# The low halves of the expert rows of three batches: from a GpSimd subtraction to a TensorE difference that ScalarE copies out

## The reference, cut to what matters

```python
h = h + attention(layernorm(h))                     # 4 x 384 x 192
x2 = layernorm(h)                                   # the expert rows
logits = x2.reshape(1536, 192) @ router_w.T         # 8 experts
probs = softmax(logits); topk_probs, topk_idx = top_k(probs, 2)
u = silu(einsum('th,eih->tei', x2, w1)); outs = einsum('tei,ehi->teh', u, w2)
h = h + sum over the two chosen experts of outs * balanced weight
```

## Time and profile before

| what | value |
|---|---|
| time, median of 3 runs | 314.09 us (311.51 to 314.11) |
| the profiled execution | 313.65 us |
| its span, first to last instruction | 311.9 us |
| what lies around the span | 1.75 us |
| mean granted TensorE clock | 0.911 |
| TensorE busy | 241.0 us (77%) |
| VectorE busy | 213.9 us (69%) |
| ScalarE busy | 178.5 us (57%) |
| GpSimd busy | 114.9 us (37%) |

### The profile page before, as it was taken

One profiled execution on the slowest core, in us unless ns is written; L12 is line 12 of the kernel. 1 busy time (PEld: TensorE's weight loads), 2 busy tenths in 40 slices (PEclk: granted clock), 3 DMA queues, 4 the chain that ended last, 5 costly groups with the idle time before them and its releaser, 6 DMA issues.

```text
span 311.9 us, 7415 instructions
## 1 busy us (share of the span) xinstructions
PE 241.0 (77%) x2435; PEld 173.0 (55%) x2436; DVE 213.9 (69%) x650; ACT 178.5 (57%) x418; POOL 114.9 (37%) x150
## 2 busy tenths in 40 slices
PE   2896977486675878898979987399999999999400
PEld 1365357243444556675667776147777677777300
DVE  2076777789998756867969999556566566566546
ACT  1167035167878989897897265045565456555222
POOL 5000005134453033030403031556768677773400
PEclk9999997569999799899899999569999999999955
DMA  6992001400000000303000021112122111110076
GB/s 173 301 246 55 2 1 30 172 1 1 3 0 3 0 2 2 104 2 103 3 2 30 14 64 49 35 48 61 61 62 72 47 62 54 42 38 32 5 243 211
DMA packets 13390, 19.01 MB, mean 61 GB/s; under 512 B 3451, under 2 KB 11138, under 8 KB 12850
## 3 DMA queue, kind: packets, MB, share of 16 engines
q1 hardware_dynamic: 10018, 13.90, 14.8%
q0 software_dynamic: 3024, 4.73, 5.1%
q10 hardware_dynamic: 320, 0.01, 0.1%
HBM read 14.69 MB, written 5.41 MB: 64 GB/s over the span
## 4 chain that ended last, share of the span: by engine, by line
PE 42%; DVE 25%; ACT 14%; DMA 6%; issue 6%; SPq 4%; POOL 1%; DVEq 0%; POOLq 0%; ACTq 0%
PE bank L989 4%; PE bank L1002 3%; PE bank L1004 3%; PE bank L1003 3%; DMA qk<-in_w1b 3%; PE bank L974 3%; DVE third_place L1426 3%; PE bank L978 2%; PE bank L976 2%; PE bank L977 2%; PE bank L975 2%; PE bank L960 2%; ACT at_half L1156 2%; DMA v<-y_rows 2%; PE bank L651 2%
## 5 line engine op out<-in xcount | busy, mean ns | idle before, releaser
L1239 ACT ACTIVATE qk<-bank 128x512 f32<-128x512 f32 x31 | 18.5, 597 | 49.6 <-PE bank L978 49.6
L564 POOL DMA_INDIRECT qk<-x_rows,tok_row x32 | 34.5, 1078 | 19.4 <-issue 8.8
L571 POOL DMA_INDIRECT y_rows<-qk,dst_row x31 | 31.4, 1011 | 20.2 <-DVE qk L1792 13.4
L1002 PE MATMUL bank<-wx,qk 128*128 x124 | 30.5, 246 | 0.6 <-DVE qk L1786 0.5
L1004 PE MATMUL bank<-wx,qk 128*128 x124 | 30.5, 246 | 0.0
L1003 PE MATMUL bank<-wx,qk 128*128 x124 | 30.5, 246 | 0.0
L1786 DVE COPY qk<-bank 128x512 f16<-128x512 f16 x31 | 13.2, 425 | 24.8 <-PE bank L989 24.8
L1476 DVE SCALAR_TENSOR_TENSOR at_half<-bank,at_half 128x384 f16<-128x384 f32 x48 | 25.1, 548 | 4.4 <-ACT at_half L1156 4.2
L1780 DVE TENSOR_TENSOR qk<-qk 128x512 f16<-128x512 f32 x31 | 21.4, 692 | 7.9 <-ACT qk L1240 7.9
L1156 ACT ACTIVATE at_half<-bank 128x384 f16<-128x384 f32 x48 | 21.3, 511 | 2.8 <-PE bank L802 2.8
L989 PEld LDWEIGHTS bank<-ident,qk 128*128 128x128 f16 x248 | 16.6, 99 | 7.7 <-DVE qk L1780 1.1
(11 more groups left out here) (317 smaller groups left out, 706.2 us busy)
## 6 DMA issues: line engine op xcount, KB each, us to landing
early<-in_w SPq DMA_DIRECT2D x4, 768.0 KB, 4.6
qk<-in_w1a SPq DMA_DIRECT2D x2, 1024.0 KB, 6.2
qk<-in_w1b SPq DMA_DIRECT2D x4, 512.0 KB, 10.2
x_rows<-xr SPq DMA_DIRECT2D x4, 288.0 KB, 2.3
v<-y_rows SPq DMA_DIRECT2D x4, 288.0 KB, 4.9
qk<-y_rows SPq DMA_DIRECT2D x4, 288.0 KB, 5.3
out<-hr SPq DMA_DIRECT2D x4, 288.0 KB, 2.7
at_half<-in_wq SPq DMA_DIRECT2D x1, 704.0 KB
```

The lines of the kernel that those rows point to most:

```text
L564: pool.indirect_dma_start(xg[:, i % 4, :], None, x2_dram, bass.IndirectOffsetOnAxis(ap=tok_row[:, i:i + 1], axis=0), bounds_check=NTOK - 1 ...
L571: pool.indirect_dma_start(y_dram, bass.IndirectOffsetOnAxis(ap=dst_row[:, i:i + 1], axis=0), ye[:, i % 4, :], None, bounds_check=2 * NTOK ...
L1002: pe.matmul(o_, actT[:, k, 0, c], w[:, W2H + d:W2H + d + D], start=(m == 0), stop=False)
```

## The change

Only the low halves of batches 1 to 3 are formed in another way. Batch 0 stays on GpSimd.

- VectorE writes a negative identity `minus16` once, at `t == 1` of the attention loop.
- TensorE has `rows_low(b)`: into banks 6 and 7 of PSUM it multiplies the float32 rows by the float32 identity, and adds the high half times the negative identity. It waits for ScalarE's high halves, and from batch 2 on for ScalarE's copy of the batch ahead.
- ScalarE has `rows_low(b)`: it copies both banks as float16 into the low columns of `xr`. Its order becomes: high 1, high 2, low 1, low 2, high 3, the exponential, low 3, clear `xg`.
- The two runs of 50 matmuls of `keep_busy` become 24 + 14 and 20 + 18, around the new ones, and write to bank 2 instead of bank 7.
- SyncE waits for ScalarE's copies for batches 1 to 3.

```diff
@@ SyncE
-                sp.wait_ge(s_xlo_ready, 2 * (b + 1))
+                if b == 0:
+                    sp.wait_ge(s_xlo_ready, 2)
+                else:
+                    sp.wait_ge(s_xdiff_ready, 2 * b)
@@ GpSimd
-            for b in range(1, B):
-                rows_low(b)
@@ TensorE
-            keep_busy(50)
+            def rows_low(b):
+                pe.wait_ge(s_xhi_ready, 2 * (b + 1))
+                if b >= 2:
+                    pe.wait_ge(s_xdiff_ready, 2 * (b - 1))
+                xrow, xf = xr[:, b % 2 * CT:(b % 2 + 1) * CT, :], x2[:, b % 2, :, :]
+                for bk, w, c0, h0 in ((6, P, 0, 0), (7, D - P, P, 2 * P)):
+                    place = bank[bk][:, 0:CT * w].rearrange("p (c d) -> p c d", d=w)
+                    pe.matmul(place, ident[:], xf[:, :, c0:c0 + w], start=True, stop=False)
+                    mm = pe.matmul(place, minus16[:], xrow[:, :, h0:h0 + w], start=False, stop=True)
+                mm.then_inc(s_xdiff_mm, 1)
+
+            keep_busy(24, 2)
+            rows_low(1)
+            keep_busy(14, 2)
...
-            keep_busy(50)
+            rows_low(2)
+            keep_busy(20, 2)
+            rows_low(3)
+            keep_busy(18, 2)
             pe.wait_ge(s_colb_ready, 1)
@@ ScalarE, rows_high
-                if b >= 2:
-                    act.wait_ge(s_xlo_ready, 2 * (b - 1))
+                if b == 2:
+                    act.wait_ge(s_xlo_ready, 2)
@@ ScalarE
-            for b in range(1, B):
-                rows_high(b)
+
+            def rows_low(b):
+                act.wait_ge(s_xdiff_mm, b)
+                xrow = xr[:, b % 2 * CT:(b % 2 + 1) * CT, :]
+                act.activation(xrow[:, :, P:2 * P], bank[6][:, 0:CT * P].rearrange("p (c d) -> p c d", d=P), ACT.Copy).then_inc(s_xdiff_ready, 1)
+                act.activation(xrow[:, :, P + D:2 * D], bank[7][:, 0:CT * (D - P)].rearrange("p (c d) -> p c d", d=D - P), ACT.Copy).then_inc(s_xdiff_ready, 1)
+
+            rows_high(1)
+            rows_high(2)
+            rows_low(1)
+            rows_low(2)
+            rows_high(3)
             act.wait_ge(s_ls_ready, 1)
             act.activation(ex, ex, ACT.Exp).then_inc(s_ex_ready, 1)
+            rows_low(3)
             act.wait_ge(s_rank_mm, 1)
@@ VectorE
                 if t == 1:
+                    dve.tensor_scalar(minus16[:], ident16[:], -1.0, None, ALU.mult)
                     dve.memset(keep, 1.0)
```

More of the change, by code:

```diff
@@ L112, in build @@
         ident16 = sb("ident16", [P, P], F16)
+        minus16 = sb("minus16", [P, P], F16)
         ident_b = sb("ident_b", [P, P], BF16)
@@ L316, in build @@
         s_xlo_ready = sem("xlo_ready")
+        s_xdiff_mm = sem("xdiff_mm")
+        s_xdiff_ready = sem("xdiff_ready")
         s_x2_stored = [sem(f"x2_stored{i}") for i in range(2)]
@@ L777, in _, with keep_busy @@
                     params(t - 2)
-            def keep_busy(n):
+            def keep_busy(n, bk=7):
                 for _ in range(n):
-                    pe.matmul(bank[7][:, 256:512], ident16[:], w_half[:, 0, 0, 0:256], start=False, stop=False, skip_group_check=True)
+                    pe.matmul(bank[bk][:, 256:512], ident16[:], w_half[:, 0, 0, 0:256], start=False, stop=False, skip_group_check=True)
             def masked_scores(t, half):
```

## The result

| | before | after |
|---|---|---|
| median of 6 runs each | 314.1 us (311.51 to 314.92) | 311.2 us (308.73 to 313.67) |
| ratio after / before | | 0.988, 95% interval 0.983 to 0.992 |
| profiled execution, its span | 313.65 us, 311.9 us | 310.51 us, 308.7 us |

Every ratio in this document leaves out the runs that lie over 1.5% above the fastest of their kernel, two of the six of the changed kernel here. The mean over all six is 311.28 against 313.87, 2.6 us less. So the change gains 1.9 to 2.6 us by the means and 3.8 us by the ratio. I had forecast 1.6 us, within the 1% that I said a measurement can tell from no change.

What follows compares the result with a forecast made beforehand. VectorE was taken to stand still 3.0 us while GpSimd subtracts; TensorE's queue would leave 1.6 us of gain. 313.65 − 1.6 = 312.05 us, forecast as 312.5 us because the median lay 0.44 above the profiled run; range 310.3 to 314.7.

Steps and rivals of the forecast that it cites:

- VectorE's excess ahead of the ranks: Before the rank matmuls, VectorE instructions held by GpSimd's subtractions of batches 1 and 2 would shorten, saving 2.0 us.
- lost to TensorE's queue at the ranks: Rank matmuls wait behind TensorE's 14 keep_busy matmuls until 184.80 us, 1.0 us later than they could start.
- excess behind the ranks: After the rank matmuls, VectorE's L1725 and L1728, held by batch 3's subtractions, would shorten, saving 1.0 us.
- one-hot matmuls later than VectorE: TensorE ends the one-hot matmuls at 194.6 us, while VectorE alone would reach L1745 at 194.14.
- X: TensorE's time for one batch's low-half difference, two float32 and two float16 matmuls: 1.15 to 1.4 us, taken as 1.28.
- 190.74 + 3X: Time in us when TensorE finishes the one-hot matmuls; one difference's TensorE time X enters three times; break-even at X = 1.81.
- The clock rival: Expert loop starts earlier but the clock rises no earlier, so 0.8 us of gain is lost: 313.3 us, chance 0.16.
- The full gain of 2.8 us: Rival: TensorE's difference takes near 0.51 us, VectorE is last again at the one-hot matmuls: 311.3 us, chance 0.08.
- The costly queue: Rival: third difference and 18 keep_busy matmuls delay the one-hot matmuls, 2.3 us later than before: 316.4 us, chance 0.06.
- The negative identity: Rival: VectorE's new minus16 instruction in the attention loop is held by GpSimd, gain only 0.7 us: 313.4 us, chance 0.10.
- The store of the rows: Ahead of the first gather, the last row store lands at 194.9 us, leaving 0.4 us slack before the row numbers.

Runs made afterwards that it cites:

- the kernels with 5 and 7 fillers: Changed kernel with 5 or 7 instead of 14 keep_busy matmuls ahead of the rank matmuls: medians 310.4 and 311.2 us, ratios to before 0.991 and 0.995.

## Why the prediction was wrong

The direction, the mechanism (VectorE is held, TensorE's queue takes part of the gain back) and the places were right; the size was too small. By its own steps, with the profiles of before and after:

| step | forecast | measured |
|---|---|---|
| VectorE's excess ahead of the ranks | 2.0 us | 1.87 (selection's end, L1692 or L1722, after the start of the stage: 6.32 before, 4.45 after) |
| lost to TensorE's queue at the ranks | 1.0, so L1716 comes 1.04 earlier | 0.56, so 1.31 (7.49 and 6.18 us into the stage) |
| excess behind the ranks | 1.0 | 0.99 (L1716 to the end of L1741: 9.19 before, 8.20 after) |
| one-hot matmuls later than VectorE | 0.46 | 0.03 (from L1741's end to L1745: 0.03 before, 0.06 after) |
| sum | 1.6 us | 2.27 us |

**The step that failed** is the one on the rank matmuls: "They take 1.08 us (185.84 to 186.92)", and with it "The rank matmuls start at 184.80, 1.0 us later than they could". The 1.08 us were read from an execution in which TensorE was early, and they hold a wait: L939 cannot start before the scan L1695 has ended. In before the scan ends at 186.18 and L939 starts at 186.24, in the timelines of VectorE and TensorE of before:

```profile
185.82 0.36 DVE L1695 TENSOR_TENSOR_SCAN third_place<-third_place 128x96 f32<-128x96 f32 x1
```

```profile
186.24 0.39 PE L939 MATMUL bank<-third_place,ones 128*128 128x8 f32 x2
```

The profile showed no idle there, because the records of pipelined matmuls overlap, and the order rows in this document had the wait (`sums_ready`). A TensorE that comes late finds the sums ready, and takes 0.80 us (182.84 to 183.64). The start itself was forecast right (5.33 us into the stage, measured 5.34). The duration was 0.28 us too long, and this made 1.04 us of the 1.31 by which L1716 came earlier. So the queue cost 0.56 us and not 1.0: the kernels with 5 and 7 fillers show the floor at 5.62 us into the stage. The forecast of the run without low halves had the same fault.

**The second mis-sized term** is the time from the ranks to the end of the one-hot matmuls, 9.8 us in the forecast (184.80 to 194.6) and 9.00 in after (182.84 to 191.84). The next difference starts 0.64 us behind the ranks' start, not 1.08: 0.44 us, and the same misread 1.08 again. The 24 one-hot matmuls take 0.76 us, not 1.0: 0.24 us. The other 0.12 us are spread over small terms. One of them was right by luck: ScalarE's copies take 0.60 us and not 0.8, but start 0.20 us after the difference is through (184.72 to 184.92), a handover that the forecast had at nothing. X itself was right: 1.32 us against 1.28, and its threefold weight was confirmed. The doubled X checks the total: with 2.29 us the formula 190.74 + 3X puts TensorE 1.4 us behind before's 196.18, and the stage was only 0.64 us longer than before's: the forecast's constant was 0.8 us too large, as these terms say.

**The rest.** The part of the measured difference beyond 2.27 us is not of the stage. The likeliest source is the two groups of executions, unevenly met by few runs. The 29 runs of before lie in two heaps, 7 at 311.3 to 312.0 us and 22 at 313.0 to 315.1, and the four profiled ones fit them (311.74 us with the early rise, 313.65 to 314.37 with the late one). Of the six in the result one is in the lower heap, while three of the changed kernel's six are at 308.7 to 310.5. Most runs have no profile that would tell their group, so this is argued and not shown.

**The clock rival came in part.** What lies behind the row numbers took 116.07 us in after and 115.00 in before, and there the two profiles differ in the clock. The expert loop's first matmuls start at 196.59 in after and at 200.80 in before. From there until it rises (206.9 and 208.4) the clock is at 1.2 GHz, 0.50 in the third column from the right; first after, then before:

```profile
196.60:206.90 10.30, 8.76 (x35) 4.21 (x36) 4.87 (x10) 2.77 (x5) 6.33 (x6) 0.50 0.20 59
```

```profile
200.80:208.40 7.60, 6.22 (x26) 2.94 (x27) 3.57 (x7) 1.83 (x4) 4.45 (x4) 0.50 0.26 67
```

The loop came 4.2 us earlier and the rise only 1.5 us, so 2.7 us more of the loop ran at the lower level. At half rate that costs at most 1.35 us, an estimate from these rows, and 1.07 us were lost. That is what the rival described, with a price near its 0.8. It was in the forecast as a chance of 0.16 and not in the sum. The 14 profiles agree in the main. In the six where this rise comes 13.3 to 14.2 us behind the row numbers, the rest takes 115.6 to 116.4 us, and in the eight where it comes 7.3 to 12.7 us behind them, 114.7 to 115.5. It is not in proportion (114.87 us for the 7.3). Both profiles of the changed kernel are among the six (116.07 and 115.62 us), and those with fewer fillers among the eight (115.12, 114.71 and 114.87). Whether the change itself brings the late rise or these executions happened to have it is open; no run was made for it.

**The rivals.** The full gain of 2.8 us needed a small X and did not come; with 5 fillers the stage does gain 2.83 us. The costly queue did not come; doubling X made it, and turned the gain of the stage into a loss of 0.64 us. The negative identity did not wait. The store of the rows was no limit: the last was issued at about 190.1 us and takes 2.3, to 192.4, and the row numbers came at 192.67, so its slack is down to 0.3 us, near the 0.4 forecast.

## What to carry to other kernels

A GpSimd instruction off the critical path can still be paid for in full on it, when it reads memory while VectorE works with two inputs; look for short VectorE instructions that end together with a GpSimd one beside them. When a duration is taken from a group of instructions in a trace, look at each of them for a wait of its own, above all where the engine was early, since pipelined records hide it. And where the effect is about 1%, compare the length of the changed stage over several profiles: here it repeated to 0.01 us, while whole executions spread over 4 us.

## What the runs showed of the hardware

- A one-input instruction can be held as well: L1725 (tensor_scalar, float32 to float16) took 0.87 us beside a subtraction. Beside a memset of GpSimd the same instruction (L1729 there) took 0.19 us, although it started 0.12 us into it. L1728 in that run, float32 to float32, took 0.27 instead of 0.18 us beside a memset. The rows don't say why a reading GpSimd instruction holds an instruction with one input.
- Reductions were not held: L1688 with the subtractions twice took 0.24 us, between two instructions that were.
- GpSimd is slowed as well: beside VectorE's long two-input instructions its subtraction of 128x384 took 1.77 instead of 0.92 us.
- Executions of one kernel come in two groups, 1.7 to 2.9 us apart at 180 us, told apart by when the granted clock first rises (40.8 to 45.4 us, or 32.8 to 33.8) and so by how many matmuls TensorE gets through between 33 and 41 us (21 or 22, or 36 to 39).
